# A band-matrix preparation moved between stages, and one engine's order of work in the modulation stage

## The reference, cut to what matters

```python
x = x + window_attention(_ln_c(x))                 # attention stage
t = t + mixture_of_experts(_ln_t(t))               # expert stage: 8 experts, the best 2 of each token
# layer 1: focal modulation
y = _ln_c(x) @ Wf + bf                             # focal input stage: q, ctx (128 channels each), 4 gates
for l, k in enumerate((k0, k1, k2)):               # depthwise 3x3, 5x5, 7x7      } convolution
    ctx = gelu(dwconv_same(ctx, k))                #                              } stage
    ctx_all = ctx_all + ctx * gates[..., l:l + 1]  #                              }
ctx_all = ctx_all + gelu(mean(ctx)) * gates[..., 3:]
m = q * (ctx_all @ Wh + bh)                        # modulation stage (focal output)
x = x + (layernorm(m) * gamma + beta) @ Wp + bp
t = t + recurrent(_ln_t(t))                        # 3136 sequential steps: recurrent stage
```

## Time and profile before

| | us |
|---|---|
| three runs | 10211.29, 10199.72, 10208.51 |
| median | 10208.51 |
| profiled execution: its time, its span | 10199.94, 10198.2 |
| attention stage, from the trace | to about 1835 |
| expert stage | 1845 to 3855 |
| focal input stage | 3861 to 4523 |
| convolution stage | 4534 to 6387 |
| modulation stage | 6396 to 8324 |
| recurrent stage | 8329 to 10192 |

### The profile page before, as it was taken

One profiled execution on the slowest core, in us unless ns is written; L12 is line 12 of the kernel. 1 busy time (PEld: TensorE's weight loads), 2 busy tenths in 40 slices (PEclk: granted clock), 3 DMA queues, 4 the chain that ended last, 5 costly groups with the idle time before them and its releaser, 6 DMA issues. The chain is left out here.

```text
span 10198.2 us, 326079 instructions
## 1 busy us (share of the span) xinstructions
PE 8869.0 (87%) x109727; PEld 5616.9 (55%) x109727; DVE 6418.7 (63%) x21703; ACT 4565.8 (45%) x12677; POOL 5604.3 (55%) x6830
## 2 busy tenths in 40 slices
PE   8999999789998996868999999677777778888888
PEld 6777777444444444644555555466666665555554
DVE  8999999799999997854555555444444442222222
ACT  5666666455555556863333333233333333333333
POOL 7888888688887886751222222233333344444444
PEclk9999999999999998989999999666666669999999
DMA  1222222111111116874444443544444422222222
GB/s 52 58 58 58 58 58 58 50 55 51 51 55 51 51 53 183 269 226 149 160 147 160 160 149 122 123 110 108 103 106 111 110 64 56 56 56 57 56 56 54
DMA packets 798452, 960.02 MB, mean 94 GB/s; under 512 B 323883, under 2 KB 662636, under 8 KB 774381
## 3 DMA queue, kind: packets, MB, share of 16 engines
q1 hardware_dynamic: 798060, 956.25, 32.8%
HBM read 576.90 MB, written 455.45 MB: 101 GB/s over the span
## 5 line engine op out<-in xcount | busy, mean ns | idle before, releaser
L945 PE MATMUL moe_pe_out<-moe_we,moe_xnT 128*128 128x512 f32 x3136 | 1573.8, 625 | 188.9 <-DVE moe_acc L839 147.9
L1550 PE MATMUL conv_pc<-conv_c,conv_toep 128*128 128x432 f32 (+1 forms) x3584 | 1371.2, 535 | 0.0
L1412 POOL TENSOR_TENSOR conv_g<-conv_c,conv_gate 128x896 f32<-128x896 f32 x128 | 365.6, 2857 | 1475.8 <-DVE conv_out L1513 1370.8
L2112 ACT ACTIVATE rec_yT<-rec_ph 128x32 f32<-128x32 f32 x3136 | 618.6, 197 | 1241.7 <-PE rec_ph L2233 1241.7
L945 PEld LDWEIGHTS moe_pe_out<-moe_we,moe_xnT 128*128 128x128 f32 x3136 | 544.9, 195 | 1047.5 <-issue 1041.0
L741 ACT ACTIVATE moe_scaled<-moe_pe_out,moe_gate 128x128 f32<-128x128 f32 x3136 | 884.8, 377 | 507.0 <-PE moe_pe_out L945 505.2
L1719 POOL TENSOR_TENSOR mod_rstd<-mod_var,mod_halfneg 112x8 f32<-112x8 f32 x226 | 372.4, 1648 | 1240.2 <-DVE mod_var L1823 1238.2
L2233 PE MATMUL rec_ph<-rec_yT,rec_vt 128*32 128x32 f32 x25080 | 842.8, 207 | 196.5 <-ACT rec_yT L2112 121.8
L1550 PEld LDWEIGHTS conv_pc<-conv_c,conv_toep 128*128 128x128 f32 x3584 | 671.7, 190 | 602.6 <-issue 602.6
L2159 DVE COPY rec_xT<-rec_pin 128x512 f32<-128x512 f32 x196 | 135.4, 691 | 1241.0 <-PE rec_pin L2205 1241.0
L282 POOL TENSOR_SCALAR att_xn<-att_xin,att_mv,att_rstd 128x128 f32<-128x128 f32 x1024 | 869.7, 860 | 54.3 <-POOL att_rstd L278 54.3
(11 more groups left out here) (202 smaller groups left out, 21330.0 us busy)
## 6 DMA issues: line engine op xcount, KB each, us to landing
conv_toep<-rows_dram SPq DMA_DIRECT2D x32, 2304.0 KB, 14.0
c<-foc_cs SPq DMA_DIRECT2D x32, 1856.0 KB, 15.6
conv_cin<-c SPq DMA_DIRECT2D x32, 1856.0 KB, 9.0
ctx_all<-conv_out SPq DMA_DIRECT2D x32, 1792.0 KB, 6.6
att_xin<-x_windows SPq DMA_DIRECT2D x512, 98.0 KB
x<-att_x1s SPq DMA_DIRECT2D x1024, 49.0 KB
moe_xin<-x SPq DMA_DIRECT2D x112, 448.0 KB, 3.5
x<-moe_acc SPq DMA_DIRECT2D x112, 448.0 KB, 2.7
```

The costliest lines, as they stand in the source:

```text
L945: pe.matmul(pe_out[:, b, half, :], xnT[:, n.slot(2), t, :], we[:, half * 4:half * 4 + 4, :].rearrange("d e c -> d (e c)"), start=True, sto ...
L1550: ins = pe.matmul(pc[k][:, half, 0:HALF * wide].rearrange("p (b i) -> p b i", i=wide)[:, :, i0:i1], w, tile[:, b, i0 + away:i1 + away], st ...
L2112: act.activation(yT[:, a, cs], ph[:, a, cs], ACT.Sigmoid).then_inc(moved, 1)
```

## The change

Three things change.

1. In the modulation stage PE's step n does the same four things in another order: `project(n+1)`, `modulator(n+10)`, `gram_of(n-3)`, `turn_context(n+11)`.
2. The taps are spread in the expert stage: POOL zeroes `gvec` there, SP loads the taps in step 1, stores the table in step 2, copies the rows of groups 0 and 1 in step 3, and expands them in steps N-5 and N-4, ahead of these steps' loads. SP waits for the expansions at the stage's end. The convolution stage begins with the gate table, then loads groups 0 and 1; from group 2 on it is as before.
3. In the expert stage ACT's `shares(n+1)` stands behind `pick` of tile 3 instead of tile 2.

```diff
 def expert_stage(...)
+        gvec = S.sb("gvec", [C, G_ALL])
...
+            def taps(first, last):
+                if first == 1:
+                    sp.wait_ge(taps_zero, 1)
+                    load_taps(sp, gvec, kernels, taps_in)
+                if first == 2:
+                    sp.wait_ge(taps_in, 16 * sum(TAPS))
+                    sp.dma_start(gvec_dram, gvec[:]).then_inc(gvec_out, 16)
+                if first == 3:
+                    sp.wait_ge(gvec_out, 16)
+                    sp.dma_start(dram(group_dram, 0, [(G_ALL, 2 * QUAD), (1, G_ALL)]),
+                                 dram(gvec_dram, 0, [(G_ALL, 2 * QUAD), (1, G_ALL)])).then_inc(group_in, 16)
+                if last in (-5, -4):
+                    sp.wait_ge(group_in, 16)
+                    expand_taps(sp, group_dram, rows_dram, last + 5, rows_made)
+
             def step(n, first, last):
+                taps(first, last)
                 if first == 0:
                     for k in range(3):
                         load(n + k)
...
+            sp.wait_ge(rows_made, 16 * 6)
...
             pool.memset(halfneg[:], -0.5).then_inc(filled, 1)
+            pool.memset(gvec[:], 0.0).then_inc(taps_zero, 1)
...
-                        if t == 2:
+                        if t == 3:
                             shares(n + 1)
...
+def load_taps(eng, gvec, kernels, sem):
+    for k, size in enumerate(TAPS):
+        r = size // 2
+        at = G_OFF[k] + P - 1 + FURTHEST[k] - r * ROW - r
+        for row in range(size):
+            eng.dma_start(gvec[:, at + row * ROW:at + row * ROW + size],
+                          dram(kernels[k], row * size, [(size * size, C), (1, size)])).then_inc(sem, 16)
+
+def expand_taps(eng, group_dram, rows_dram, s, sem):
+    for k, blocks in enumerate(BLOCKS):
+        eng.dma_start(dram(rows_dram, s * QUAD * P * T_ALL + T_OFF[k], [(P * T_ALL, QUAD), (T_ALL, P), (1, P * blocks)]),
+                      dram(group_dram, s * QUAD * G_ALL + G_OFF[k] + P - 1,
+                           [(G_ALL, QUAD), (-1, P), (1, P * blocks)])).then_inc(sem, 16)
...
 def convolution_stage(...)
         @block.sync
...
                 if first < PER:
-                    make_rows(g)
-                    make_rows(g + 1)
-                    load(g)
-                    load(g + 1)
+                    load(g, 0)
+                    load(g + 1, 1)
...
 def focal_output_stage(...), PE's step
+                if last < -1:
+                    project(n + 1, first + 1)
                 if last < -10:
                     modulator(n + 10, first + 10)
+                if first >= 3:
+                    gram_of(n - 3, first - 3, last - 3)
                 if last < -11:
                     turn_context(n + 11, first + 11)
-                if last < -1:
-                    project(n + 1, first + 1)
-                if first >= 3:
-                    gram_of(n - 3, first - 3, last - 3)
```

More of the change, by code:

```diff
@@ L544, in _, with expert_stage @@
             run_steps(pe, N, U // 2, step)
-def expert_stage(nc, B, x1, router_w, router_b, expert_w, expert_b, erank, ident, x2):
+def expert_stage(nc, B, x1, router_w, router_b, expert_w, expert_b, erank, ident, x2, kernels, gvec_dram, group_dram, rows_dram):
     T = 7
@@ L616, in expert_stage @@
         x2_out = S.sems("x2_out", 4)
+        taps_zero, taps_in, gvec_out, group_in, rows_made = (S.sem(k) for k in ("taps_zero", "taps_in", "gvec_out", "group_in", "rows_made"))
         block = S.block()
@@ L1287, in _, with convolution_stage @@
             run_steps(pe, N, U, step, AHEAD)
-def convolution_stage(nc, B, c0, gates, kernels, gap_mask, ctx_all):
+T_ALL = P * sum(BLOCKS)
+T_OFF = (0, P * BLOCKS[0], P * (BLOCKS[0] + BLOCKS[1]))
+def load_taps(eng, gvec, kernels, sem):
[10 more added lines that the diff above has]
+                           [(G_ALL, QUAD), (-1, P), (1, P * blocks)])).then_inc(sem, 16)
+def convolution_stage(nc, B, c0, gates, gap_mask, ctx_all, gvec_dram, group_dram, rows_dram):
     N = C
@@ L1301, in convolution_stage @@
     AHEAD = 4
-    T_ALL = P * sum(BLOCKS)
-    T_OFF = (0, P * BLOCKS[0], P * (BLOCKS[0] + BLOCKS[1]))
     S = Stage(nc, "conv")
     with S.ctx:
-        gvec = S.sb("gvec", [C, G_ALL])
         ones = S.sb("ones", [P, P])
@@ L1328, in convolution_stage @@
         zeroed = S.sem("zeroed")
-        taps_in, gvec_out = S.sem("taps_in"), S.sem("gvec_out")
         const_in = S.sem("const_in")
@@ L1344, in _ @@
         def _(sp):
[L1345 to L1351, removed]
             sp.dma_start(gate[:], gates).then_inc(const_in, 16)
             sp.dma_start(gap[:], gap_mask).then_inc(const_in, 16)
-            sp.wait_ge(taps_in, 16 * sum(TAPS))
-            sp.dma_start(gvec_dram, gvec[:]).then_inc(gvec_out, 16)
-            sp.wait_ge(gvec_out, 16)
             def make_rows(g):
@@ L1362, in make_rows, with load @@
                              dram(gvec_dram, g.val(PER * G_ALL), [(G_ALL, PER), (1, G_ALL)])).then_inc(group_in[s], 16)
[L1363 to L1369, removed]
+                hold(sp, group_in[s], g.turn(2, 16), ticks)
+                expand_taps(sp, group_dram, rows_dram, s, rows_made[s])
+            def load(g, first):
                 s = g.slot(2)
@@ L1374, in load @@
                   .then_inc(c0_in[s], 16)
-                hold(sp, rows_made[s], g.turn(2, 48, 48), ticks)
+                if first >= 2:
+                    hold(sp, rows_made[s], g.turn(2, 48), ticks)
                 sp.dma_start(toep[:, s, :, :], dram(rows_dram, s * PER * P * T_ALL, [(T_ALL, P), (P * T_ALL, PER), (1, T_ALL)]))\
@@ L1391, in step @@
                     hold(sp, convolved[2], n.val(1, 1), ticks)
-                    load(g + 2)
+                    load(g + 2, 2)
                 hold(sp, combined, n.val(1, 1), ticks)
@@ L1402, in _ @@
         def _(pool):
-            pool.memset(gvec[:], 0.0).then_inc(zeroed, 1)
             pool.memset(ones[:], 1.0).then_inc(zeroed, 1)
@@ L1417, in _ @@
         def _(act):
-            act.wait_ge(zeroed, 2)
+            act.wait_ge(zeroed, 1)
             act.wait_ge(const_in, 32)
@@ L1525, in _ @@
         def _(pe):
-            pe.wait_ge(zeroed, 2)
+            pe.wait_ge(zeroed, 1)
             def convolve(k, n, first, group_first):
@@ L2286, in metaformer_program @@
     gram = scratch("gram", C, C + 1)
+    taps = scratch("gvec_dram", C, G_ALL), scratch("group_dram", 2, QUAD, G_ALL), scratch("rows_dram", 2, QUAD, P, T_ALL)
     attention_stage(nc, B, a["x_windows"], a["w_qkv_t"], a["w_proj_t"], a["b_proj"], a["rpb_rev"],
                     a["shift_mask"], a["ident"], x1)
-    expert_stage(nc, B, x1, a["router_w"], a["router_b"], a["expert_w"], a["expert_b"], a["erank"], a["ident"], x2)
+    expert_stage(nc, B, x1, a["router_w"], a["router_b"], a["expert_w"], a["expert_b"], a["erank"], a["ident"], x2,
+                 [a["k0"], a["k1"], a["k2"]], *taps)
     focal_input_stage(nc, B, x2, a["Wf"], a["bf"], a["ident"], q, c0, gates)
-    convolution_stage(nc, B, c0, gates, [a["k0"], a["k1"], a["k2"]], a["gap_mask"], ctx_all)
+    convolution_stage(nc, B, c0, gates, a["gap_mask"], ctx_all, *taps)
     focal_output_stage(nc, B, ctx_all, q, x2, a["Wh"], a["bh"], a["gamma"], a["beta"], a["Wp"], a["bp"],
```

3 lines of the change are left out of this document (removed).

## The result

| | before | after |
|---|---|---|
| median of four runs, us | 10207.59 | 9434.38 |
| profiled execution: time, span, us | 10199.94, 10198.2 | 9429.81, 9428.0 |
| mean granted clock | 0.91 | 0.965 |

A forecast was written before the change was run, and what follows sets the result against it. Modulation was taken as bound by a ring of PE and DVE waiting for each other. 10200 - 590 (modulation) - 64 (taps) + 40 (expansions) - 3 (shares) = 9583, stated as 9590 us; own range 9490 to 9690, 8-in-10 range 9490 to 9780.

The forecast's parts named there:

- The two serialise: Modulation, old order: modulator waits for DVE's gate behind the projection's mean, projection stands behind modulator; 8.48 us a step.
- that wait goes: Modulation: with projection issued a step earlier, PE's modulator no longer waits for DVE's gate, 2.09 us a step.
- 4.7 us ... I take 4.8: Modulation, new order: ring of turning, ACT's copy, square and normalisations, gram sets the step; 4.8 us at full clock.
- + 17 + 158 + 20: Modulation, us beside the steps: 17 for projection's wait at image starts, 158 for DVE's loop turnovers, 20 for loads.
- DVE's 4.2: Modulation: DVE and POOL's step, 3.93 us mean to mean plus 0.3 for negation and second variance; such steps save 720.
- Full speed nearly throughout: Modulation: long-streaming work side by side and the shorter step bring full clock nearly throughout; likely, not certain.
- Rival A: Modulation: clock stays at 1.2 GHz, steps of 7.4 us, 140 us saved there, 10,033 us in all; 7%.
- the tail's row: Modulation's last steps, only projections and grams: PE busy 48.65 of 50 us yet granted 0.50; evidence for a low clock.
- rival B: Modulation: clock goes up and down or loads come late, mean step about 6.1 us, -315, 9858 us; 16%.
- The taps out of the convolution, -64: Convolution start: without the chain of taps and expansions PE starts 64.7 us earlier; taken as 64, from 50 to 69.
- The expansions in the expert stage, +40: Expert stage: loads behind two expansions make DVE wait 19 us twice, plus 2 for PE's clock; 0 to 71.
- The shares, -3: Expert stage: ACT's shares moved behind its fourth tile; DVE is the bound, same work; -3 us, between -31 and +20.

The follow-up runs named there:

- run 1: PE's new order in the modulation alone, on the kernel before: 9498.89 us, ratio 0.9298.
- run 7: The changed kernel with PE's turning of the next context before the gram instead of behind it: 9300.97 us, ratio 0.9128.
- run 6: The kernel before, in its old order, with four zero-adding products behind the gram in each modulation step: 9816.12 us, ratio 0.9608.
- Run 2: The kernel before with only the taps spread and the first two expansions made in the expert stage: 10163.57 us, ratio 0.9959.
- run 3: The kernel before with only ACT's shares one tile later: 10167.51 us, ratio 0.9965.
- run 5: The kernel before with POOL's pair sums over 8 of 128 columns and ACT's shares one tile later: 10021.51 us, ratio 0.9810.

## Why the prediction was wrong: sizes in the modulation, mechanism in the shares

- **"The two serialise", "that wait goes".** Right. The ring was the one named; opening it and the clock that came with it gave 695 us, with the order alone (run 1).
- **"4.7 us ... I take 4.8".** The ring was the right one, the term mis-sized: 4.49 us. The gram counted 1.1 and the turning 0.7 in the sum, where in the ring they are 0.97 (6726.51 to 6727.48) and 0.62, and 0.1 was added as caution. 214 x 0.31 = 66 us of the miss. By itself this would have left 9524, inside the own range.
- **"+ 17 + 158 + 20".** Over the 1119 us of the first window 214 steps of 4.49 leave 158 for turnovers, image starts and loads together; 195 was forecast: 37 us. That it is no more is luck, for the terms miss in opposite directions. Fourteen steps with a turnover among them take 75.4 us from mean to mean, without one 68.1. Twelve turnovers at 7.3 us are 88 us, where 15 at 10.5 were forecast (158). An image start costs 2.6 us, as its two distances are 6.23 and 5.38 instead of 4.49 each; 30 of them are some 79 us, where 17 was forecast. (That makes 167 and not 158: 214 steps are 213 distances, and the first few take 3.9 us.) The mechanism was named, projection waiting for ACT's square (43.5 us in 28 waits); its size was taken as 0.55 us an image. The loads, 20 in the sum, show no wait in this window.
- **DVE's 4.2.** It bounded nothing here, but its 0.3 us for two operations was wrong (run 7): DVE's step is 3.9. Run 7 saves 834 us against before where the bound by DVE's chain was 720.
- **The clock.** "Full speed nearly throughout" came nearly so: 0.90, which with two levels is four fifths of the time at 2.4 GHz. Rival A (7%), which lived from the tail's row, and rival B (16%), which rested on the 0.63, are out; run 6 shows that a higher clock in the old ring was worth 377 us by itself. The tail's row itself still stands. In the changed kernel the last modulator ends at 7503.9, and only projections and grams follow. The granted clock is full until 7525.6 and 0.50 from there on, while PE is busy for 17.35 of 18 us (7526 to 7544); the 0.77 of the longer window is a mean of the two. So that row holds for such steps in both orders, and says nothing of steps with modulator and turning. The Trainium skill (TensorE: Matmul & The Clock Gate, Part 1) says that an engine kept busy is released to 2.4 GHz; the changed kernel's stretch agrees (0.90), the tails of both kernels don't (0.50).
- **The taps out of the convolution, -64.** Measured -66: right.
- **The expansions in the expert stage, +40.** Run 2 measured 36, with waits of 16.6 and 14 us where two of 19 were forecast. Right, and slightly high.
- **The shares, -3.** Wrong: -36 (run 3). The prediction took DVE to be the bound and "gets the same work". It does, but the same instructions were shorter. Its own bound of -31 came close by luck: it was taken from ACT's idle share, which was worth nothing in run 5; the term that mattered was the length of 784 additions, which it had named and left unpriced. 33 us of the miss.
- Stages that the change doesn't touch are 7 us shorter together, as two executions may differ.

Together 66 + 37 + 33 + 4 + 2 + 7 = 149 us, of the 156 by which 9434 differs from 9590; the rest is rounding in the sum and the distance of the profiled execution from the median. The failed steps are thus three: the ring's 4.8 us a step (4.49 measured), the 195 us beside it (158), and the shares taken at -3 because DVE "gets the same work" (-36). They have the same sign: after the first the sum is at 9524, after the second at 9487, just below the own range, after the third at 9454. The ring's sum carried rounding up at three places in one direction.

## What to carry to other kernels

Take a ring's terms as starts to starts from one row of the timeline, at the clock expected, and add no caution to them: per-step rounding is multiplied by the number of steps. Check each term beside the ring by itself afterwards: here two large misses nearly cancelled. Where DVE is the bound, compare the mean length of its SBUF-to-SBUF additions with their shortest before saying that moving another engine's work is free. After opening a ring, ask at once what the new last link is; here moving one more link (turning before gram) gave another 133 us, and cutting a wait that lay beside a later one gave nothing.

## What the runs showed of the hardware that was not expected

- Four products per step that add zeros made the kernel 385 us faster: the granted clock of the modulation went from 0.63 to 0.96. PE's busy share was 75% in both windows (1369 of 1815 us, 1030 of 1370), so the busy share didn't show what was to be had. In the last steps of the stage it is 96 to 97% at 0.50, in both kernels.
- POOL's sums of 761 and 464 ns stretch DVE's additions from 286 to 411 and 397 ns on average; shortening them takes 178 us off the expert stage.
- DVE stands idle for 6.8 us ahead of its first instruction when the 14-step body turns over (12 times), and moving the loads beside it hardly changes that (6.4).
